# Scaled keys and values ahead of a delta-rule scan, copy-only helpers inside it, and a token copy placed later in an expert loop

## The reference

```python
q = _l2norm((xc @ wq).reshape(b, t, H, HD))      # 16 heads of 16
k = _l2norm((xc @ wk).reshape(b, t, H, HD))
v = (xc @ wv).reshape(b, t, H, HD)
beta, alpha = sigmoid(xc @ wb), sigmoid(xc @ wa + 4.0)
def step(S, (q_, k_, v_, b_, a_)):               # one token
    S = a_ * S
    pred = einsum('bhkv,bhk->bhv', S, k_)
    S = S + k_[:, None] * (b_ * (v_ - pred))[None, :]
    o = einsum('bhkv,bhk->bhv', S, q_)
...
x = layernorm(x + attention block); x = layernorm(x + cross attention over ctx)
expert = argmax(x @ Wr + br)
x = layernorm(x + gelu(gelu(x @ W1 + b1) @ W2 + b2) @ W3 + b3)   # of that expert
```

## Time and profile before

| | |
|---|---|
| median of the runs | 2067.56 us |
| the profiled execution | 2071.13 us |
| its span, first to last instruction | 2069.5 us |
| DVE busy | 1328.2 us (64%) |
| PE busy | 1419.1 us (69%) |
| POOL busy | 999.8 us (48%) |
| ACT busy | 755.0 us (36%) |

### The profile page before, as it was taken

How to read it: one execution, slowest core, us unless ns; L and a number is a source line. 1 busy time by engine, 2 the same in 40 slices (tenths; PEclk the granted TensorE clock), 3 DMA queues, 4 the chain that set the end, 5 groups by cost and what they waited for, 6 DMA issues and landing times. The chain is left out here.

```text
span 2069.5 us, 28474 instructions
## 1 busy us (share of the span) xinstructions
PE 1419.1 (69%) x6660; PEld 983.3 (48%) x6661; DVE 1328.2 (64%) x3231; ACT 755.0 (36%) x2412; POOL 999.8 (48%) x1213
## 2 busy tenths in 40 slices
PE   6424448400025666676775899998669999999997
PEld 5313336300024455455554677776535555555554
DVE  4699999999989999999878124334323232223232
ACT  5511114401102555564676377776401111111111
POOL 3267777776668877777567523432111111111111
PEclk9756779855558878787886999999779999999998
DMA  4501114600031000010000212142240320320300
GB/s 125 196 11 31 42 32 132 239 0 0 0 128 35 20 25 18 23 34 24 25 25 16 97 35 60 40 128 75 69 128 21 120 90 20 131 84 21 101 18 6
DMA packets 97685, 125.41 MB, mean 61 GB/s; under 512 B 10001, under 2 KB 74952, under 8 KB 95560
## 3 DMA queue, kind: packets, MB, share of 16 engines
q1 hardware_dynamic: 60040, 97.22, 14.8%
q10 hardware_dynamic: 33136, 18.58, 3.1%
q0 software_dynamic: 4432, 8.73, 1.2%
HBM read 89.68 MB, written 35.74 MB: 61 GB/s over the span
## 5 line engine op out<-in xcount | busy, mean ns | idle before, releaser
L210 POOL TENSOR_TENSOR wt<-wt 128x1024 f32<-128x1024 f32 x128 | 301.1, 2352 | 152.0 <-DVE wt L168 152.0
L216 POOL TENSOR_TENSOR wt<-wt 128x512 f32<-128x512 f32 (+2 forms) x384 | 322.6, 840 | 30.1
L1846 PE MATMUL e_ph<-wt,e_g 128*128 x624 | 274.4, 593 | 0.0
L168 DVE SCALAR_TENSOR_TENSOR wt<-wt,scan 128x256 f32<-128x256 f32 x512 | 241.5, 472 | 0.1
L158 DVE TENSOR_TENSOR scan<-scan,wt 128x256 f32<-128x256 f32 x512 | 220.3, 430 | 19.7 <-DVE wt L168 14.1
L149 DVE TENSOR_REDUCE scan<-wt 128x16 f32<-128x272 f32 x512 | 222.2, 434 | 0.1
L1244 ACT ACTIVATE wt<-p_pX,p_mx 128x120 f32<-128x120 f32 x512 | 176.0, 379 | 101.9 <-DVE p_mx L1089 101.6
L137 DVE TENSOR_TENSOR wt<-wt,scan 128x256 f32<-128x256 f32 x512 | 208.6, 407 | 4.7 <-PEq L233 4.7
L1375 PE MATMUL p_pm<-p_w_mix,p_oT 128*128 128x256 f32 x128 | 43.9, 502 | 240.7 <-DMA p_oT<-o 210.0
L1739 POOL TENSOR_TENSOR e_ve<-e_mv,eps 128x1 f32<-128x1 f32 x39 | 7.4, 189 | 375.4 <-DVE e_mv L1790 375.4
L1846 PEld LDWEIGHTS e_ph<-wt,e_g 128*128 128x128 f32 x624 | 115.6, 190 | 130.8 <-issue 130.8
(11 more groups left out here) (212 smaller groups left out, 2987.6 us busy)
## 6 DMA issues: line engine op xcount, KB each, us to landing
wt<-in_L_ffn_W SPq DMA_DIRECT2D x24, 1024.0 KB, 5.3
qkv<-f_st ACTq DMA_DIRECT2D x48, 256.0 KB, 2.3
p_kE<-kE SPq DMA_DIRECT2D x16, 480.0 KB, 3.7
p_vP<-vP SPq DMA_DIRECT2D x16, 480.0 KB, 4.5
e_xt<-routed ACTq DMA_DIRECT2D x39, 130.0 KB, 2.1
f_xt<-in_x SPq DMA_DIRECT2D x16, 256.0 KB, 3.0
f_raw_k<-qkv SPq DMA_DIRECT2D x4, 1024.0 KB, 5.2
f_raw_q<-qkv SPq DMA_DIRECT2D x4, 1024.0 KB, 7.9
```

Of the source, the lines that this page charges most:

```text
L168: nc.vector.scalar_tensor_tensor(s["S"][:, h, u], s["S"][:, h, (u - 1) % R], s["gate"][:, jb, h, 1, bass.ds(c * R + u, 1)], s["outer"][:], ...
L210: nc.gpsimd.tensor_tensor(x, s["S"][:, h, z * Q:(z + 1) * Q], s["q"][:, h, now].rearrange("p t (o d) -> p t o d", o=1).to_broadcast([P, Q, ...
L216: nc.gpsimd.tensor_tensor(x[:, :, :, 0:half], x[:, :, :, 0:half], x[:, :, :, half:2 * half], ALU.add).then_inc(s["o_fold"][h], 1)
L1846: ins = nc.tensor.matmul(ph2[:], g1[:, c // (C1 // 2), c % (C1 // 2)], wt[:, bass.ds(at_b + (W2_AT + c * F2), F2)], start=(c == 0), stop=( ...
```

## The change

Per half and h, two more factors are made once: `gain` = sqrt(beta alpha) and `share` = -beta / gain. The reciprocal length of the keys is multiplied by gain (so that the stored keys carry it), and the values are multiplied by share in place. The scan's key helper then is a plain copy from SBUF to PSUM; the value helper multiplies by a one that is broadcast from one PSUM column; and the state update subtracts the outer product instead of adding it. The order of the parts changes: ACT makes the gates before the roots, takes the root of beta alpha (`gain_root`) and then that of the lengths; for h = 0 of the first half, ACT makes only the gates inside the projection pipeline, and both roots after it. DVE makes `gates` ahead of `inverse`, and adds `shares`. In the first scan's last two chunks the five parts come after steps 1, 2, 4, 6 and 7. In the experts, the two waits and the token copy move behind the first-layer biases.

```diff
-        ("nab", (JB, 2, TB)),
+    s["one"] = bank[:, 511:512]
-def next_keys(nc, s, jb, t):
-    nc.vector.tensor_tensor(s["kn"][:], s["k"][:, :, bass.ds(t, KN)],
-                            s["nab"][:, jb, :, bass.ds(t, KN)]...to_broadcast([P, 2, KN, HD]), ALU.mult)
+def next_keys(nc, s, t):
+    nc.vector.tensor_copy(s["kn"][:], s["k"][:, :, bass.ds(t, KN)]).then_inc(s["kn_done"], 1)
 def next_values(...):
     nc.vector.tensor_tensor(s["sk"][:, :, u:u + n, :, HD], vo[:, :, :, bass.ds(t, n)].rearrange("p h d t -> p h t d"),
-                            s["gate"][:, jb, :, 0, bass.ds(t, n)]...to_broadcast([P, 2, n, HD]),
+                            s["one"].rearrange("p (x y z) -> p x y z", x=1, y=1).to_broadcast([P, 2, n, HD]),
                             ALU.mult).then_inc(s["v_done"], 1)
@@ state_update
-                                   ALU.mult, ALU.add).then_inc(s["S_done"], 1)
+                                   ALU.mult, ALU.subtract).then_inc(s["S_done"], 1)
@@ lengths, DVE
                 def gates():
                     dve.wait_ge(gate_done, 2 * (p + 1))
-                    nc.vector.scalar_tensor_tensor(s["nab"][:, jb, h], beta, -1.0, alpha, ALU.mult, ALU.mult)
+                    if jb:
+                        dve.wait_ge(share_done, shared(h, VALUED))
+                    nc.vector.tensor_tensor(gain[:, h], beta, alpha, ALU.mult).then_inc(both_done, 1)
+                def shares():
+                    dve.wait_ge(root_done, rooted(p, GAIN))
+                    nc.vector.reciprocal(share[:, h], gain[:, h]).then_inc(share_done, 1)
+                    dve.wait_ge(share_done, shared(p, SHARE))
+                    nc.vector.scalar_tensor_tensor(share[:, h], beta, -1.0, share[:, h], ALU.mult, ALU.mult)
+                    dve.wait_ge(raw_in["v"][h], 16 * (jb + 1))
+                    dve.wait_ge(share_done, shared(p, SIGNED))
+                    v = values[jb][:, h]
+                    nc.vector.tensor_tensor(v, v, share[:, h]...to_broadcast([P, HD, TB]), ALU.mult)
                 def inverse():
-                    dve.wait_ge(root_done, p + 1)
+                    dve.wait_ge(root_done, rooted(p, ROOT))
                     nc.vector.reciprocal(rn[:, h], roots[:, h]).then_inc(rn_done, 1)
+                    dve.wait_ge(rn_done, inverted(p, INVERSE))
+                    nc.vector.tensor_tensor(rn[:, h, 0], rn[:, h, 0], gain[:, h], ALU.mult).then_inc(rn_done, 1)
-                return partial(sums, 0), partial(sums, 1), inverse, gates
+                return partial(sums, 0), partial(sums, 1), gates, inverse, shares
@@ DVE, before the first scan, for each h
+            gates()
             inverse()
             for i in range(2):
                 normalise(0, 0, i)
-            gates()
+            shares()
@@ DVE, last two chunks of the first scan
-                    if u % 2:
+                    if u in (1, 2, 4, 6, 7):
                         parts.pop(0)()
@@ lengths, ACT
+                def gain_root():
+                    act.wait_ge(both_done, p + 1)
+                    nc.scalar.activation(gain[:, h], gain[:, h], ACT.Sqrt, bias=tiny[:, 0:1]).then_inc(root_done, 1)
-                return partial(square, 0), partial(square, 1), root, gates
-            pipeline(act, M, 3, ..., between={M - 2: keys, M - 1: queries, M: root})
-            for part in (set_gates, *lengths(0, 1)):
+                return partial(square, 0), partial(square, 1), gates, gain_root, root
+            pipeline(act, M, 3, ..., between={M - 2: keys, M - 1: queries, M: set_gates})
+            for part in (gain_root, root, *lengths(0, 1)):
@@ experts, DVE: the first three instructions of part a move behind its last
-                    dve.wait_ge(x_in[s], m * 16 + 16)
-                    if since(n, 2):
-                        dve.wait_ge(row_out[s], m * 16)
-                    nc.vector.tensor_copy(token[:, s], xt[:, s, D:D + 1]).then_inc(token_kept, 1)
                     dve.wait_ge(xT_done, n + 1)
                     nc.vector.tensor_copy(xT[:], pX[:]).then_inc(xT_out, 1)
 ...
                         nc.vector.tensor_tensor(h1[:, q], ph1[:, q], wt[...], ALU.add).then_inc(h1_out, 1)
+                    dve.wait_ge(x_in[s], m * 16 + 16)
+                    if since(n, 2):
+                        dve.wait_ge(row_out[s], m * 16)
+                    nc.vector.tensor_copy(token[:, s], xt[:, s, D:D + 1]).then_inc(token_kept, 1)
```

More of the change, by code:

```diff
@@ L108, in scan_state, with next_values, scan_start @@
     return s
[L111 to L118 removed]
+def next_keys(nc, s, t):
+    nc.vector.tensor_copy(s["kn"][:], s["k"][:, :, bass.ds(t, KN)]).then_inc(s["kn_done"], 1)
+def next_values(nc, s, vo, t, u, n):
     nc.vector.tensor_tensor(s["sk"][:, :, u:u + n, :, HD], vo[:, :, :, bass.ds(t, n)].rearrange("p h d t -> p h t d"),
[L121 removed]
+                            s["one"].rearrange("p (x y z) -> p x y z", x=1, y=1).to_broadcast([P, 2, n, HD]),
                             ALU.mult).then_inc(s["v_done"], 1)
[L125 to L128 removed]
+def scan_start(nc, s, vo):
+    next_keys(nc, s, 0)
+    next_values(nc, s, vo, 0, 0, V)
 def state_product(nc, dve, s, jb, c, u, h):
@@ L256, in front_and_scan @@
         lens, roots, rn = shaped(arena(4 * TB), (2, 2, TB)), sb("roots", [P, 2, 2, TB]), sb("rn", [P, 2, 2, TB])
-        alpha_bias, len_eps = sb("alpha_bias", [P, 1]), sb("len_eps", [P, 1])
+        alpha_bias, len_eps, tiny = (sb(n, [P, 1]) for n in ("alpha_bias", "len_eps", "tiny"))
+        gain, share = sb("gain", [P, 2, TB]), sb("share", [P, 2, TB])
         wk, wv = (wkv[:, i * G * D:(i + 1) * G * D].rearrange("p (g n) -> p g n", g=G) for i in range(2))
@@ L281, in front_and_scan @@
         gate_in = [sem(f"f_gate_in{h}") for h in range(2)]
-        gate_done, nab_done, sq_done, fold_done, root_done, rn_done, norm_done = (
-            sem("f_" + n) for n in ("gate_done", "nab_done", "sq_done", "fold_done", "root_done", "rn_done",
-                                    "norm_done"))
+        gate_done, both_done, share_done, sq_done, fold_done, root_done, rn_done, norm_done = (
+            sem("f_" + n) for n in ("gate_done", "both_done", "share_done", "sq_done", "fold_done", "root_done", "rn_done", "norm_done"))
+        GAIN, ROOT = 1, 2
+        INVERSE, SCALED = 1, 2
+        SHARE, SIGNED, VALUED = 1, 2, 3
+        rooted = lambda p, what: 2 * p + what
+        inverted = lambda p, what: 2 * p + what
+        shared = lambda p, what: 3 * p + what
         cT_done, cT_out, k_done, v_done, kE_done, vP_done = (
@@ L288, in front_and_scan @@
         NSMALL, NW = 4, 5
-        SETUPS = 12
+        SETUPS = 13
         TAPS = KC * G
@@ L432, in _ @@
             nc.vector.tensor_scalar(parity[:, 0:1], parity[:, 1:2], -1.0, 1.0, ALU.mult, ALU.add).then_inc(parity_done, 1)
+            nc.vector.memset(s["one"], 1.0).then_inc(parity_done, 1)
             dve.wait_ge(small_in, 16 * NSMALL)
@@ L490, in normalise @@
                 dve.wait_ge(raw_in[name][h], 16 * (jb + 1))
-                dve.wait_ge(rn_done, jb * 2 + h + 1)
+                dve.wait_ge(rn_done, inverted(jb * 2 + h, SCALED))
                 nc.vector.tensor_tensor(dst[:, h], src[:, h].rearrange("p d t -> p t d"),
                                         rn[:, h, i].rearrange("p (t o) -> p t o", o=1).to_broadcast([P, TB, HD]), ALU.mult).then_inc(norm_done, 1)
-            keys, queries, inverse, gates = lengths(0, 0)
+            keys, queries, gates, inverse, shares = lengths(0, 0)
             pipeline(dve, M, 2, step, between={M - 1: keys, M: queries})
@@ L503, in _ @@
                 normalise(0, 0, i)
-            gates()
-            keys, queries, inverse, gates = lengths(0, 1)
+            shares()
+            keys, queries, gates, inverse, shares = lengths(0, 1)
             keys()
             queries()
+            gates()
             inverse()
@@ L510, in _ @@
                 normalise(0, 1, i)
-            gates()
+            shares()
             dve.sem_inc(s["S_done"], 2)
-            for h in range(2):
-                dve.wait_ge(raw_in["v"][h], 16)
-            dve.wait_ge(nab_done, 2)
+            dve.wait_ge(share_done, shared(1, VALUED))
             dve.wait_ge(norm_done, 4)
-            scan_start(nc, s, 0, values[0])
+            dve.wait_ge(parity_done, 4)
+            scan_start(nc, s, values[0])
             scan_chunk(nc, dve, s, 0, values[0], 0)
@@ L532, in _ @@
                 normalise(1, h, 1)
-            for h in range(2):
-                dve.wait_ge(raw_in["v"][h], 32)
-            dve.wait_ge(nab_done, 4)
+            dve.wait_ge(share_done, shared(3, VALUED))
             dve.wait_ge(norm_done, 8)
-            scan_start(nc, s, 1, values[1])
+            scan_start(nc, s, values[1])
         @block.scalar
@@ L635, in root @@
                     nc.scalar.activation(roots[:, h], lens[:, h], ACT.Sqrt, bias=len_eps[:, 0:1]).then_inc(root_done, 1)
-                return partial(square, 0), partial(square, 1), root, gates
```

(7 more changed lines are left out.)

9 lines of the change are left out of this document (6 added, 3 removed).

## The result

The changed kernel takes 2014.47 us (median of 4 runs, 2012.56 to 2016.74) against 2069.53 us before; the ratio is 0.9731, interval 0.9716 to 0.9747. That is 55 us less; 46 were forecast, 2021.5 us in a range of 2005 to 2037. The profiled execution took 2012.56 us, span 2010.9, so the two profiles lie 58.6 us apart, as each lies on the outer side of its median.

What follows compares the result with a forecast made beforehand. DVE was taken to bound both scans and PE the stretch from 1137 us on; -32.5 - 32.6 + 12.4 + 7.4 + 3.5 - 4 = -46 us, from 2067.56 to 2021.5 us, range 2005 to 2037.

Steps and rivals of the forecast that it cites:

- What bounds the kernel: Both scans: DVE sets the pace, and the excess of helper lines L120 and L113 is a wait for POOL's instruction in progress.
- The first scan's helpers: First scan: L120's 63 instances lose 36.1 us of duration, counted at 0.9, so -32.5 us; L113 is already free.
- The second scan's helpers: Second scan, 587 to 1005 us: L120 and L113 lose 38.4 us, counted at 0.85, so -32.6 us; nothing counted later.
- the passing on: Rival: DVE waits for POOL in other products or for a ring slot; 16 us more, 2037.5 us; chance 0.14.
- Before the first scan: Ahead of the first scan: later roots, `shares` and extra table loads delay the start by 12.4 us, ends 10 and 14.
- The last two chunks: First scan's last two chunks: key products and `shares` between scan steps add 7.4 us, ends 5 and 12.
- The turn: Between the scans: `shares` of h = 1, partly under POOL's folds, adds 3.5 us, ends 0 and 6.
- Experts: Experts: with the token copy behind the biases, PE's waits for the transposed input go, -4 us, ends 0 and -5.
- The signs: New profile: L120 near 260 ns, L113 near 290, first helper near 119 us, first scan about 430, tiles 13.6 us apart.

Runs made afterwards that it cites:

- the square of four runs: Changed kernel, value helpers' one in PSUM or SBUF, small routing results in SBUF or PSUM: 2014.5 and 1996.5 us (one in PSUM), 2070.2 and 2063.8 (one in SBUF).

## Why the prediction was right, step by step

*What bounds the kernel.* Right: the second SBUF operand, and POOL's instruction in progress, explain the excess of the helpers (91 long helpers, each ending with a POOL instruction), and one operand's place takes away or brings back 55.7 us. The estimated 65 ns more that a PSUM operand might have cost, which the prediction left out, aren't there: the medians are 258 and 259 ns, and the free ones of the kernel before lay at 251 to 267.

*The first scan's helpers.* Forecast -32.5 on durations of 36.1. L120's 52.5 us became 16.4, exactly 36.1; the helpers alone shortened this scan by 31.6 us. The first 14 chunks, where nothing else changed, give the factor: durations of both helpers 35.2 us less, the stretch 31.8 less (377.1 to 345.3), 0.90 as forecast. Right.

*The second scan's helpers.* The total (-30.7 against -32.6) is nearly right, its make-up isn't, and that is luck. Over the first 13 chunks the durations of the helpers fell by 36.9 us (51 and 26 of them, 39.5 + 18.1 to 13.2 + 7.5), about as forecast, but the stretch shrank by only 25.4 (416.3 to 390.9): a factor of 0.69, where I took 0.85. The routing products took the difference: five groups of small products and one copy, with SBUF operands alone, grew by 8.3 us in those chunks, and from 23.2 to 39.4 us over the whole scan. I had named the passing on as a rival with half the gain; it holds in part, as the square of four runs shows too. On the other side, I counted nothing behind that point, and 5.3 us came there (133.8 to 128.5): the last chunks did shrink, as DVE's idle time there fell from 23 to 14 us.

*Before the first scan.* Forecast +12.4, found +10.8, and the front ahead of it ran 1.2 us earlier in this execution, so +12.0. The single terms hold: the root's delay, `shares`, and the folds of h = 1 that begin once h = 0 is done.

```profile
81.07 1.28 ACT L655 ACT_TABLE_LOAD   x1
...
83.19 1.75 DVE L502 RECIPROCAL f_rn<-f_roots 128x256 f32<-128x256 f32 x1 [6.28 <-ACT f_roots L659]
...
93.84 2.29 DVE L486 TENSOR_TENSOR f_vo<-f_vo,f_share 128x2048 f32<-128x2048 f32 x1
...
104.84 1.75 DVE L502 RECIPROCAL f_rn<-f_roots 128x256 f32<-128x256 f32 x1 [1.09 <-ACT f_roots L659]
```

DVE idles 6.3 us ahead of the first reciprocal, the price of the roots' place, which the run with the roots early takes back in part.

*The last two chunks.* Forecast +7.4. New work there was some 5 us (L480, L482 and L486 of h = 0 took 5.5, the products of gains 1.3 where one signed product had taken 2.3, the key products 0.6), and the folds lost 6.7 us of waiting (20.2 to 13.5), which I hadn't foreseen: their new places relative to POOL's instructions seem luckier, which wasn't tried by itself. So the two chunks shrank by 2.4 us (76.2 to 73.8) instead of growing by 7.4 less the helpers' part. This is most of the 9 us by which the first scan, and the sum of the medians, came out better than forecast. It is luck: nothing in the prediction's working led there.

*The turn.* Forecast +3.5, found +1.5: POOL's first folds lasted 7.6 us instead of 12.2, its next two instructions 8.9 us instead of 2.6.

*Experts.* Forecast -4, found -5.7: 4.5 in the stalls and 1.2 in the last tile.

*The signs.* The helpers' means and tails, the keys' 288 ns, the first helper (117.8 us) and the tiles' distance came as named. Three did not: the first scan took 419 us, not 430; the stretch to the last step with two chunks shrank by 25.4 us, not 33; and one wait of PE for the transposed input is left. Of the two that were to show the prediction wrong, the first (a mean above 600 ns) didn't come. The second was that other DVE products with SBUF operands grow by more than 15 us together. The routing's grew by 16.2 us in the second scan, so by itself that group passes the mark; the folds of the first scan fell by 6.7, which leaves 9.5. The time came right all the same, because the folds, the last chunks and the experts gave more than was counted.

## What to carry to other kernels

A short VectorE instruction with a mean far above its shortest instance, beside a busy GpSimd, is waiting inside its own duration, where no list of idle time shows it: compare min, median and max by line. For a product, one operand in PSUM takes it out of the wait, even if that means multiplying by a one; the output in PSUM alone doesn't (mean 658 ns). For a copy, the output in PSUM does it; a copy within SBUF waits. What such waits are worth together isn't the sum of the durations: count each stretch by its span and go through all such products, since those left over take up part of what is won until they too are moved.

## What the runs showed of the hardware

A copy of 64 elements with one SBUF input and an SBUF output waits for GpSimd as a product of two SBUF operands does (median 873 ns, shortest 226), and a copy of 128 elements into PSUM doesn't at all (285 to 295 ns in 64 instances). A VectorE product with one PSUM operand isn't dearer than one from SBUF: 250 ns against 256 for the shortest at 64 elements. The 91 value helpers of the kernel before that lasted over 400 ns each ended 120 to 132 ns after the GpSimd instruction that was in progress when they began. A GpSimd product of 0.30 us can last 3.3 us behind one VectorE product. Taking the waits from three small products and a copy had two outcomes: with the helpers free, another product that nobody had touched fell from 2.1 us to 0.2 in the steady step; with the helpers waiting, the two totals grew by 3.4 us over the second scan.
